# A one-core macaron block on Trainium2: GpSimd's wide SBUF operations handed to VectorE, and attention's side work spread over the query tiles

## The chip, the cores and the metric

One core of one Trainium2 chip. The metric is device time in microseconds (us) of one launch, median of several runs. The engines are TensorE (PE, with its weight loads PEld), VectorE (DVE), ScalarE (ACT), GpSimd (POOL) and SyncE (SP, which here only issues DMAs). Each engine runs its own list of instructions in order and waits on semaphores.

## The reference, cut to what matters

```python
x = x + 0.5 * ffn(layernorm(x))        # x: 4 batches x 1024 tokens x 128
x = x + attn(layernorm(x))
x = x + 0.5 * ffn(layernorm(x))
# ffn(t): logits = t Wr' + br over 8 experts; the best two, softmax of the two -> w
#         o_e = relu(t W1_e' + b1_e) W2_e' + b2_e;  result = LN(t + sum_e w_e o_e) * gamma + beta
# attn(n): q12 = n w_q12, k12 = n w_k12, v = n w_v
#          diff = softmax(q1 k1' s) - lam * softmax(q2 k2' s);  o = diff v;  o / rms(o) * 0.2
```

All is float32. The kernel computes only the two chosen experts of each token: the rows are scattered by expert into a buffer in HBM and multiplied in tiles of 128 rows.

## The kernel before, in words

A batch is 1024 tokens, held as 8 tiles of 128 (TB = 8). The program has five stages: routing of the first feed-forward (normalise rows, logits, choice of two experts, places by prefix sums, scatter of the rows by indirect DMA from POOL); the first feed-forward, 78 slots (SLOTS) of 128 rows, two groups of 39 (GSLOTS), a group holding two batches; attention over batches 0 to 3; the second feed-forward, again 78 slots; and an end that adds the results and stores them.

**A feed-forward slot** (`step`): PE transposes the rows (L842), multiplies by W1 (L850) and W2 (L860). ACT and DVE each copy half of the expert's W1 into a staging tile (L604, L1199), do half of the relus (L611, L1206), and DVE adds b2 (L1214). In the second feed-forward POOL sends each slot's result rows to HBM with an indirect DMA (`send`, L446). POOL also issues the scatters of the routed rows (`scatter`, L424), 16 to a batch. SP loads a slot's rows (`load`, L323), but those of a group only after `group_ready`: all its scatters and eight pad writes have landed. Between slots DVE takes small pieces of other work from generators (`next(...)`).

**An attention batch** (`attention(b)`, one list on each of PE, ACT and DVE, all ordered by hand). For tile i: PE computes two score matrices of 128 by 1024 (`scores`, L784 to L786, three matmuls per product); DVE takes the row maxima of each (`maxima`, L1374); ACT takes the exponentials (`probabilities`, L667), which frees the banks for the next tile's scores; DVE combines the two (`difference`, L1385); PE transposes (`turn`, L910) and ACT copies back (`dT_copy`, L641). After every four tiles PE multiplies by the keys' rows (`values`, L921) and Wv, ACT squares, POOL computes a scale (`value_scale`) and DVE adds to x (`add_values`).

Beside this, attention of batch b carries side work for its neighbours. For batch b+1: DVE merges the first feed-forward's two results per token (`merge_tiles`, tiles 0 and 1), POOL computes reciprocal roots (`rstd`, four small operations), ACT normalises, POOL multiplies by gamma and adds to x (`merge_add`, two operations on 128 by 1024), DVE takes statistics (`x_stats`, tile 5), POOL `rstd` again, ACT writes `xn` (`make_xn`), PE transposes it and multiplies by M (`turn_xn`, `multiply_M`), ACT and DVE split the products into a high and a low part (`copy_xnT`, `xnT_rest`, `copy_xm`, `xm_rest`), and then the scores of b+1 can begin. For batch b-1: `add_values(b-1, 1)` and `x_stats` in tile 4, `rstd`, `make_rows` in tile 5, transposes, logits, `choose`, `prefix` and `place` after tile 7, then POOL's scatters. For batch b+2 POOL issues 16 gathers (L435), eight of them ahead of the `rstd` that `make_rows` and `make_xn` wait for. `table(0)`, which turns the counts of batches 0 and 1 into slots, runs at the end of batch 2.

**POOL's wide operations** are four helpers, each on a whole batch (128 by 1024): `add_beta` (L416, four times in each feed-forward), `merge_add` (L462, L465), `add_tokens` (L470) and `gain` (L476). DVE waits for them through the semaphores `beta_added`, `merged`, `token_added` and `gained`.

## Time and profile before

| | us |
|---|---|
| median of three runs | 785.39 (783.78 to 787.7) |
| the profiled execution's own time | 786.02 |
| its span in the trace | 784.3 |
| busy: PE, DVE, ACT, POOL | 588.6, 518.8, 413.5, 384.9 |
| routing and first feed-forward | 0 to about 250 |
| attention | about 250 to 550 |
| second feed-forward and end | about 550 to 784 |

The trace holds one execution. A row of a timeline gives the start, the duration, the engine, the source line, the operation, output and input, the count merged into it, and in brackets how long the engine sat idle before it and what released it. Granted clock is TensorE's, 1.00 being 2.4 GHz and 0.50 being 1.2 GHz.

```profile
PE   2654599998998678976887667787989858788900
...
DVE  4654666675786786994799476853648635888726
...
POOL 6455055544453067168157313413556774666643
PEclk9955599999899999998999797998999988999965
```

These are the busy tenths in 40 slices of 19.6 us each. Attention is slices 13 to 28.

### The profile page before, as it was taken

How to read it: one execution, taken by the hardware profiler on the slowest of the kernel's cores; microseconds unless marked ns; L12 is line 12 of the kernel's file. 1: busy time of each engine (PE TensorE's matmuls, PEld its weight loads, DVE VectorE, ACT ScalarE, POOL GpSimd, SP SyncE). 2: the span in 40 equal slices, each digit the busy share in tenths (PEclk: the TensorE clock that was granted, in tenths of full speed). 3: DMA queues.
4: the chain of work that ended last, by engine and by line, in shares of the span. 5: the costliest groups of instructions: out<-in, count | busy, mean ns of one | idle time of the engine just before them, and what ended most of it. 6: DMA issues, size and time to landing. Idle time of an engine off the chain costs nothing.

```text
span 784.3 us, 16226 instructions
## 1 busy us (share of the span) xinstructions
PE 588.6 (75%) x3864; PEld 508.4 (65%) x3864; DVE 518.8 (66%) x1630; ACT 413.5 (53%) x1103; POOL 384.9 (49%) x415
## 2 busy tenths in 40 slices
PE   2654599998998678976887667787989858788900
PEld 2544599998988555554655455653988747778900
DVE  4654666675786786994799476853648635888726
ACT  3443266655556377376647644653665434646621
POOL 6455055544453067168157313413556774666643
PEclk9955599999899999998999797998999988999965
DMA  8412244324331001001000001001122321412141
GB/s 281 123 56 62 54 106 109 93 69 111 95 93 52 1 10 41 3 12 34 11 28 21 8 7 49 24 4 47 40 65 72 97 62 47 152 54 59 45 161 54
DMA packets 53677, 49.18 MB, mean 63 GB/s; under 512 B 9863, under 2 KB 45875, under 8 KB 53073
## 3 DMA queue, kind: packets, MB, share of 16 engines
q1 hardware_dynamic: 44736, 31.25, 14.6%
q0 software_dynamic: 8640, 16.87, 7.0%
q8 instruction: 35, 0.57, 0.3%
q14 instruction: 58, 0.47, 0.2%
q10 hardware_dynamic: 208, 0.02, 0.0%
HBM read 25.99 MB, written 23.02 MB: 62 GB/s over the span
## 4 chain that ended last, share of the span: by engine, by line
PE 48%; DVE 20%; issue 11%; POOL 10%; ACT 6%; DMA 3%; DVEq 1%; ACTq 0%; POOLq 0%; SPq 0%
PE banks L850 15%; PE banks L860 14%; PE banks L921 5%; PE banks L828 3%; POOL zb L435 3%; ACT rowbuf L561 2%; PE banks L842 2%; PE banks L819 2%; POOL rs L408 2%; PE banks L784 2%; POOL rows L424 2%; PE banks L786 2%; PE banks L785 2%; DVE nb L1374 1%; DVE sum_r L1241 1%
## 5 line engine op out<-in xcount | busy, mean ns | idle before, releaser
L850 PE MATMUL banks<-scratch 128*128 128x128 f32 x1248 | 174.2, 284 | 19.4 <-DVE scratch L1199 16.8
L850 PEld LDWEIGHTS banks<-scratch 128*128 128x128 f32 x1248 | 157.7, 198 | 27.0 <-issue 20.5
L860 PE MATMUL banks<-blocks,scratch 128*128 x1248 | 169.1, 280 | 0.1
L860 PEld LDWEIGHTS banks<-blocks,scratch 128*128 128x128 f32 x1248 | 156.2, 197 | 0.7 <-issue 0.5
L1206 DVE TENSOR_SCALAR scratch<-banks,blocks 128x128 f32<-128x128 f32 x312 | 95.0, 345 | 65.7 <-PE banks L850 64.5
L424 POOL DMA_INDIRECT rows<-rowbuf,slot x96 | 95.6, 996 | 67.4 <-issue 37.7
L667 ACT ACTIVATE scratch<-banks,nb 128x1024 f32<-128x1024 f32 x64 | 71.1, 1114 | 81.0 <-DVE nb L1374 80.7
L611 ACT ACTIVATE scratch<-banks,blocks 128x128 f32<-128x128 f32 x312 | 97.7, 364 | 28.5 <-PE banks L850 27.6
L598 ACT ACTIVATE scratch<-banks 128x128 f32<-128x128 f32 x156 | 43.2, 277 | 128.7 <-PE banks L842 126.4
L1374 DVE TENSOR_REDUCE nb<-banks 128x1 f32<-128x1024 f32 x64 | 76.8, 1217 | 48.1 <-PE banks L786 47.0
L446 POOL DMA_INDIRECT results<-scratch x78 | 77.7, 996 | 61.0 <-DVE scratch L1214 43.0
L435 POOL DMA_INDIRECT zb<-yrows,slot x64 | 64.8, 1012 | 53.4 <-DVE scratch L1214 25.1
L784 PE MATMUL banks<-xnTh,xmh 128*128 128x512 f32 x128 | 59.8, 467 | 36.2 <-ACT scratch L667 29.8
L1199 DVE COPY scratch<-blocks 128x256 f32 x156 | 63.4, 407 | 27.3 <-PE banks L850 18.7
L1214 DVE TENSOR_TENSOR scratch<-banks,blocks 128x128 f32<-128x128 f32 x156 | 45.0, 289 | 32.6 <-PE banks L860 23.8
L921 PE MATMUL banks<-scratch,xn 128*128 128x512 f32 x128 | 62.6, 637 | 1.5 <-ACT scratch L641 1.5
L604 ACT ACTIVATE scratch<-blocks 128x256 f32 x156 | 63.7, 408 | 0.1
L842 PE MATMUL banks<-ident,scratch 128*128 128x128 f32 x156 | 43.9, 281 | 23.5 <-issue 12.2
L784 PEld LDWEIGHTS banks<-xnTh,xmh 128*128 128x128 f32 x128 | 26.3, 205 | 48.2 <-ACT scratch L667 33.9
L424 POOL DMA_INDIRECT rows<-scratch,slot x32 | 30.5, 953 | 51.9 <-DVE scratch L1214 51.9
L786 PE MATMUL banks<-xnTh,xml 128*128 128x512 f32 x128 | 54.2, 423 | 0.0
L785 PE MATMUL banks<-xnTl,xmh 128*128 128x512 f32 x128 | 53.9, 421 | 0.0
(175 smaller groups left out, 893.0 us busy)
## 6 DMA issues: line engine op xcount, KB each, us to landing
scratch<-rows SPq DMA_DIRECT2D x156, 64.5 KB
yrows<-scratch SPq DMA_DIRECT2D x78, 64.0 KB
scratch<-results SPq DMA_DIRECT2D x3, 1024.0 KB, 7.8
rows<-padrows SPq DMA_DIRECT2D x34, 64.5 KB
x<-in_L_attn_x_dram SPq DMA_DIRECT2D x4, 512.0 KB, 6.0
scratch<-in_L_ffn_W_dram SPq DMA_DIRECT2D x1, 2048.0 KB, 19.2
out_dram<-x SPq DMA_DIRECT2D x4, 512.0 KB, 6.1
rows<-rowbuf,slot POOLq DMA_INDIRECT x96
```

The costliest lines, as they stand in the source:

```text
L424: pool.indirect_dma_start(rows[b // GB], bass.IndirectOffsetOnAxis(slot_v[:, b, j, k:k + 1], 0), rows_of(p, b)[:, j, k, :], None).then_inc ...
L435: pool.indirect_dma_start(zb[:, i * D:(i + 1) * D], None, yrows[b // GB], bass.IndirectOffsetOnAxis(slot[:, b * PAIRS + i:b * PAIRS + i + ...
L446: pool.indirect_dma_start(results, bass.IndirectOffsetOnAxis(xt_v[:, r, D:ROW].bitcast(I32), 0), ys[:, r * D:(r + 1) * D], None, bounds_ch ...
L611: ins = act.activation(hT_of(T, c), hT_at(T, c), ACT.Relu, bias=blocks[:, B1_AT + c:][:, bass.ds(at, 1)], scale=1.0)
L667: act.activation(pp, banks[:, 2 * m * 512:(2 * m + 2) * 512], ACT.Exp, bias=nb[:, 2 * i + m:2 * i + m + 1], scale=1.0, accum_out=ll[:, i:i ...
L784: pe.matmul(o, ah, bh, start=True, stop=False)
L786: return pe.matmul(o, al, bh, start=False, stop=True)
L850: ins = pe.matmul(hT_at(T, c), staged(T, c), xT_of(T), start=True, stop=True)
L860: ins = pe.matmul(y_at(T), hT_of(T, c), blocks[:, W2_AT + c * D:][:, bass.ds(at, D)], start=(c == 0), stop=(c == FC - 1))
L921: ins = pe.matmul(bank(6), xn[b % 2][:, k * D:(k + 1) * D], dT[g][:, k * QG * P:(k + 1) * QG * P], start=(k == 0), stop=(k == TB - 1))
L1206: ins = dve.tensor_scalar(hT_of(T, c), hT_at(T, c), blocks[:, B1_AT + c:][:, bass.ds(at, 1)], 0.0, ALU.add, ALU.max)
L1374: dve.tensor_reduce(nb[:, c], banks[:, 2 * m * 512:(2 * m + 2) * 512], AX_X, ALU.max, negate=True).then_inc(nb_ready, 1)
```

## The change

The four wide helpers leave POOL and run on DVE, each in two halves of 128 by 512 (`columns`), the feed-forwards' ones as generator pieces between slots. POOL's lists are reordered. In attention, side work moves: `values` of a group is issued in one piece, `add_values(b, 0)` moves into the next batch's tile 0, `add_values(b-1, 1)` and its statistics one tile earlier, `make_rows` and `make_xn` are halved over two tiles, the preparation of batch b+1 starts before tile 7's second exponential, and the logits, `choose`, `place` of batch b-1 move into batch b+1 (tiles 0 to 4); `table(0)` moves from the end of batch 2 to tile 4 of batch 3. The scores of tile 0 wait for each 512-column chunk instead of all four.

```diff
+        BETA_AT = 18
@@ POOL
-            def add_beta(p, b): ...
-            def merge_add(b): ...
-            def add_tokens(b): ...
-            def gain(b): ...
@@ POOL, first feed-forward
-                if 2 * PAIRS <= s < 2 * PAIRS + BATCHES:
-                    add_beta(0, s - 2 * PAIRS)
@@ POOL, attention
-                if b > 1:
-                    scatter(1, b - 2, range(TB))
-                if b < BATCHES - 1:
+                if b == BATCHES - 1:
+                    scatter(1, b - 3, range(10, PAIRS))
+                if after:
                     rstd(n)
                     n += 1
-                    merge_add(b + 1)
-                if b:
+                if last:
                     value_scale(b - 1, 1)
-                if b < 2:
-                    gather(b + 2, range(TB))
-                if b > 1:
-                    scatter(1, b - 2, range(TB, 2 * TB))
-                for _ in range((b > 0) + (b < BATCHES - 1)):
+                    rstd(n)
+                    n += 1
+                if after:
+                    if b < 2:
+                        gather(b + 2, range(4))
                     rstd(n)
                     n += 1
                 if b < 2:
-                    gather(b + 2, range(TB, 2 * TB))
+                    gather(b + 2, range(4, PAIRS))
+                if b == 2:
+                    scatter(1, b - 2, range(10))
+                if b == BATCHES - 1:
+                    scatter(1, b - 2)
                 value_scale(b, 0)
-            scatter(1, BATCHES - 2, range(6))
@@ POOL, second feed-forward
                 send(s)
-                if s % 2 and s < 20:
-                    i = 6 + s // 2
-                    scatter(1, BATCHES - 2, range(i, i + 1))
+                if s < PAIRS:
+                    scatter(1, BATCHES - 2, range(s, s + 1))
...
-                if s in (GSLOTS + 1, GSLOTS + 2, GSLOTS + 3, GSLOTS + 4):
-                    add_beta(1, s - GSLOTS - 1)
-                if s in (LAST_AT + 4, LAST_AT + 8):
-                    add_tokens((s - LAST_AT) // 4 - 1)
-                if s in (LAST_AT + 19, LAST_AT + 29):
-                    gain((s - LAST_AT - 19) // 10)
-            for b in range(GB, BATCHES):
-                add_tokens(b)
-            gain(2)
@@ ACT, attention
-                    probabilities(i)
+                    if last and i == 2:
+                        o_copy(b - 1, 1)
+                    if i == TB - 1:
+                        if last:
+                            copy_tgtT(a, 0)
+                        o_copy(b, 0)
+                        dT_copy(b, i - 2)
+                        if after:
+                            make_xn(b + 1, n + after + last, halves_of(1))
+                    probabilities(i, 0)
+                    if after and i == TB - 1:
+                        copy_xnT(b + 1)
+                    probabilities(i, 1)
...
+                    if b > 1 and i == 1:
+                        copy_rows(1, b - 2)
+                    if after and i in (2, 3):
+                        ins = normalise(..., n, halves_of(i - 2))
+                    if last and i in (4, 5):
+                        make_rows(1, b - 1, n + after, halves_of(i - 4))
                     if after and i == 6:
-                        make_xn(b + 1, n + after + last)
+                        make_xn(b + 1, n + after + last, halves_of(0))
@@ PE, scores
+                        if i == 0:
+                            pe.wait_ge(xmh_sb, 4 * b + 2 * m + h + 1)
+                            pe.wait_ge(xml_sb, 4 * b + 2 * m + h + 1)
@@ PE, attention
-                pe.wait_ge(xmh_sb, 4 * b + 4)
-                pe.wait_ge(xml_sb, 4 * b + 4)
...
+                    if i == TB - 1:
+                        turn(b, i - 2)
                     scores(b, i)
+                    if b > 1 and i == 0:
+                        logits(a - 1)
...
+                    if last and i == 1:
+                        values(b - 1, 1, 0)
+                        values(b - 1, 1, 1)
+                    if last and i == 2:
                         multiply_Wv(b - 1, 1)
+                    if b > 1 and i == choose_tile(b) + 1:
+                        prefix(a - 1)
...
                 multiply_Wv(b, 0)
                 if after:
-                    pe.wait_ge(xnTh_sb, b + 2)
-                    pe.wait_ge(xnTl_sb, b + 2)
+                    multiply_M(b + 1)
                 turn(b, TB - 2)
-                if after:
-                    multiply_M(b + 1)
@@ DVE
+            def add_beta(p, b):      # two pieces of 128 x 512, then beta_added
+            def gain(r):             # two pieces
+            def merge_add(b):
+                dve.wait_ge(scaled, b)
+                at_once(gain(sum_r))
+                dve.wait_ge(beta_added, b + 1)
+                for q in range(2): ... dve.tensor_tensor(x[:, c], x[:, c], sum_r[...], ALU.add)
@@ DVE, last_sums / last_add: the tokens' sum and the gain, two pieces each, ahead of the rest
@@ DVE, attention
                     maxima(i)
+                    if after and i == TB - 1:
+                        xnT_rest(b + 1)
                     if i:
                         difference(i - 1)
+                    if b > 1 and i == 0:
+                        read_logits(a - 1)
+                    if last and i == 0:
+                        add_values(b - 1, 0)
...
+                    if b > 1 and i == choose_tile(b):
+                        at_once(choose(a - 1))
-                    if last and i == 4:
+                    if last and i == 3:
                         add_values(b - 1, 1)
                         x_stats(b - 1, n)
+                    if b > 1 and i == choose_tile(b) + 2:
+                        at_once(place(a - 1, b - 2))
+                    if b == BATCHES - 1 and i == 4:
+                        at_once(table(0))
                     if after and i == 5:
-                        dve.wait_ge(merged, b + 1)
+                        merge_add(b + 1)
                         x_stats(b + 1, n)
+                if after:
+                    xm_rest(b + 1)
                 difference(TB - 1)
...
@@ DVE, feed-forwards
+                if BETA_AT <= s < BETA_AT + 2 * BATCHES:
+                    next(first_betas)
-                    if LAST_AT + 7 + 10 * f <= s < LAST_AT + 16 + 10 * f:
+                    if LAST_AT + 5 + 10 * f <= s < LAST_AT + 16 + 10 * f:
                         next(ending[f], None)
-                    if LAST_AT + 22 + 10 * f <= s < LAST_AT + 24 + 10 * f:
+                    if LAST_AT + 20 + 10 * f <= s < LAST_AT + 24 + 10 * f:
                         next(adding[f], None)
+                if GSLOTS - 8 <= s < GSLOTS - 8 + 2 * BATCHES:
+                    next(last_betas)
```

`choose_tile(b)` is 2 for batch 2 and 0 for batch 3.

## Rows read from the trace of the kernel before

**Rows 1.** The page's part 4: shares of the chain by engine.

```profile
PE 48%; DVE 20%; issue 11%; POOL 10%; ACT 6%; DMA 3%; DVEq 1%; ACTq 0%; POOLq 0%; SPq 0%
```

**Rows 2.** Windows, one per attention batch: width, busy by engine, clock, DMA share, GB/s.

```profile
260.00:317.00 57.00, 43.70 (x197) 31.74 (x198) 45.38 (x97) 36.45 (x69) 29.64 (x29) 0.97 0.07 19
317.00:389.00 72.00, 56.43 (x257) 41.02 (x258) 54.61 (x135) 44.84 (x92) 33.18 (x36) 0.95 0.06 15
389.00:464.00 75.00, 57.63 (x257) 41.97 (x257) 56.93 (x149) 45.24 (x93) 34.27 (x36) 0.91 0.04 15
464.00:536.00 72.00, 54.39 (x245) 39.76 (x244) 49.28 (x124) 37.63 (x73) 21.27 (x26) 0.90 0.07 23
```

**Rows 3.** Timeline of DVE in attention, batches 0 and 1.

```profile
290.13 2.55 DVE L1374 TENSOR_REDUCE nb<-banks 128x1 f32<-128x1024 f32 x2
...
293.09 1.29 DVE L1385 SCALAR_TENSOR_TENSOR scratch<-scratch,cc 128x1024 f32<-128x1024 f32 x1
...
339.24 3.46 DVE L1385 SCALAR_TENSOR_TENSOR scratch<-scratch,cc 128x1024 f32<-128x1024 f32 x1
...
371.71 1.22 DVE L1374 TENSOR_REDUCE nb<-banks 128x1 f32<-128x1024 f32 x1 [10.52 <-PE banks L786]
...
392.86 2.35 DVE L1374 TENSOR_REDUCE nb<-banks 128x1 f32<-128x1024 f32 x2
```

**Rows 4.** Timeline of POOL in batch 1: the two operations of `merge_add`.

```profile
339.27 2.36 POOL L462 TENSOR_TENSOR sum_r<-sum_r,gammab 128x1024 f32<-128x1024 f32 x1 [4.35 <-ACT sum_r L561]
341.71 3.25 POOL L465 TENSOR_TENSOR x<-x,sum_r 128x1024 f32<-128x1024 f32 x1
```

**Rows 5.** Timelines of ACT (first row) and PE in attention.

```profile
361.62 3.18 ACT L561 ACTIVATE rowbuf<-x,nm,rs 128x128 f32<-128x128 f32 x8 [6.27 <-POOL nm L410]
...
260.07 0.47 PE L784 MATMUL banks<-xnTh,xmh 128*128 128x512 f32 x1 [1.50 <-DVE xml L1354]
...
364.86 1.12 PE L819 MATMUL banks<-ident,rowbuf 128*128 128x128 f32 x4 [6.01 <-ACT rowbuf L561]
```

**Rows 6.** Groups by shape: DVE's addition of 128 by 512 from two SBUF tiles.

```profile
L1339 DVE TENSOR_TENSOR x<-x,scratch 128x512 f32<-128x512 f32 x4 | 2.7, 688 | 3.7 <-issue 2.9 <-POOL scratch L476 0.7
```

**Rows 7.** Timeline of DVE in the feed-forwards, beside POOL's wide operations.

```profile
164.39 1.73 DVE L1199 COPY scratch<-blocks 128x256 f32 x1
...
665.23 2.90 DVE L1199 COPY scratch<-blocks 128x256 f32 x1
...
668.77 2.91 DVE L1199 COPY scratch<-blocks 128x256 f32 x1
...
682.34 0.61 DVE L1206 TENSOR_SCALAR scratch<-banks,blocks 128x128 f32<-128x128 f32 x2 [0.23 <-PE banks L850]
683.23 0.29 DVE L1214 TENSOR_TENSOR scratch<-banks,blocks 128x128 f32<-128x128 f32 x1 [0.28 <-PE banks L860]
683.72 0.29 DVE L1199 COPY scratch<-blocks 128x256 f32 x1 [0.20 <-PE banks L850]
...
694.38 3.42 DVE L1241 SCALAR_TENSOR_TENSOR sum_r<-zb,wts,sum_r 128x128 f32<-128x128 f32 x2
...
720.11 3.27 DVE L1241 SCALAR_TENSOR_TENSOR scratch<-scratch,wts 128x128 f32<-128x128 f32 x2
```

**Rows 8.** Timelines of PE (first, last) and POOL, second feed-forward, first group.

```profile
571.96 0.74 PE L819 MATMUL banks<-ident,rowbuf 128*128 128x128 f32 x4 [3.06 <-ACT rowbuf L561]
...
642.66 0.98 POOL L446 DMA_INDIRECT results<-scratch  x1 [0.30 <-issue]
643.94 0.97 POOL L424 DMA_INDIRECT rows<-rowbuf,slot  x1 [0.31 <-issue]
...
649.52 0.45 PE L842 MATMUL banks<-ident,scratch 128*128 128x128 f32 x1 [12.24 <-issue]
```

**Rows 9.** Timeline of the end: POOL's and DVE's operations on the last two batches.

```profile
758.26 2.33 POOL L470 TENSOR_TENSOR scratch<-scratch,tgt 128x1024 f32<-128x1024 f32 x1 [8.59 <-ACT scratch L713]
...
760.63 4.65 DVE L1241 SCALAR_TENSOR_TENSOR scratch<-scratch,wts 128x128 f32<-128x128 f32 x8 [13.58 <-POOL scratch L470]
```

More of the change, by code:

```diff
@@ L275, in macaron_kernel, with halves_of, choose_tile @@
         LAST_AT = GSLOTS + 6
+        def halves_of(tiles):
+            return range(tiles * TB // 2, (tiles + 1) * TB // 2)
+        def choose_tile(b):
+            return 0 if b == BATCHES - 1 else 2
         def wait_apart(eng, *waits):
@@ L1242, in second_result, with columns @@
                 return ins
+            def columns(b, piece, pieces):
+                n = TB * D // pieces
+                return slice(b * TB * D + piece * n, b * TB * D + (piece + 1) * n)
+            def add_beta(p, b):
+                dve.wait_ge(rows_ready, BATCHES * p + b + 1)
+                for q in range(2):
+                    xq = x[:, columns(b, q, 2)].rearrange("p (j d) -> p j d", d=D)
+                    ins = dve.tensor_tensor(xq, xq, betab[:, :].unsqueeze(1).broadcast_to([P, TB // 2, D]), ALU.add)
+                    if q:
+                        ins.then_inc(beta_added, 1)
+                    yield
+            def gain(r):
+                for q in range(2):
+                    rq = r[:, columns(0, q, 2)].rearrange("p (j d) -> p j d", d=D)
+                    steps.then(dve.tensor_tensor(rq, rq, gammab[:, :].unsqueeze(1).broadcast_to([P, TB // 2, D]), ALU.mult))
+                    yield
+            def merge_add(b):
+                dve.wait_ge(scaled, b)
+                at_once(gain(sum_r))
+                dve.wait_ge(beta_added, b + 1)
+                for q in range(2):
+                    c = columns(b, q, 2)
+                    ins = dve.tensor_tensor(x[:, c], x[:, c], sum_r[:, columns(0, q, 2)], ALU.add)
+                steps.then(ins)
             def merge_tiles(b, tiles):
@@ L1319, in last_sums @@
                 pairs = [range(j, j + 2) for j in range(0, TB, 2)]
-                dve.wait_ge(token_added, b + 1)
+                dve.wait_ge(weighted, b + 1)
+                for q in range(2):
+                    steps.then(dve.tensor_tensor(sums[b][:, columns(0, q, 2)], sums[b][:, columns(0, q, 2)], tgt[:, columns(b, q, 2)], ALU.add))
+                    yield
                 for t in pairs:
@@ L1333, in last_add @@
             def last_add(b):
-                dve.wait_ge(gained, b + 1)
-                dve.wait_ge(beta_added, BATCHES + b + 1)
-                for h in range(2):
-                    c = slice(b * TB * D + h * TB * D // 2, b * TB * D + (h + 1) * TB * D // 2)
-                    ins = dve.tensor_tensor(x[:, c], x[:, c], sums[b][:, h * TB * D // 2:(h + 1) * TB * D // 2], ALU.add)
-                    if h:
+                dve.wait_ge(scaled, BATCHES + b)
+                yield from gain(sums[b])
+                for q in range(2):
+                    c = columns(b, q, 2)
+                    ins = dve.tensor_tensor(x[:, c], x[:, c], sums[b][:, columns(0, q, 2)], ALU.add)
+                    if q:
                         ins.then_inc(x_done, 1)
@@ L1445, in _ @@
             merging = first_merge(n)
+            first_betas = itertools.chain(*(add_beta(0, b) for b in range(BATCHES)))
+            last_betas = itertools.chain(*(add_beta(1, b) for b in range(BATCHES)))
             finding = [find(b) for b in range(BATCHES)]
```

119 lines of the change are left out of this document (45 added, 74 removed).

## The prediction, made before the changed kernel ran

> **What bounds the kernel now.** I read the chain of waits first. PE holds not quite half of it, DVE a fifth, and POOL a tenth [rows 1]. POOL's tenth is the part to look at, since this change empties it. Next come the windows, one per attention batch: batch 1 lasts 72.0 us with PE busy 56.4, DVE 54.6 and POOL 33.2; batch 2 lasts 75.0 with 57.6, 56.9 and 34.3 [rows 2]. No engine is full, and two are nearly equal, so the batch pays for waits between engines. The DVE timeline shows what a tile costs when nothing waits: the two maxima start at 290.13 and the difference ends at 293.09 + 1.29 = 294.38, so 4.25 us a tile and 34 for eight [rows 3]. It also shows two holes in batch 1. DVE waits 10.52 us ahead of tile 7, and from tile 7's maxima (371.71) to the next batch's last one of tile 0 (392.86) 21.2 us go by [rows 3].
>
> The ACT and PE timelines name the first hole: ACT stood 6.27 us for POOL's `nm` before `make_rows`, and PE 6.01 us for ACT [rows 5]. POOL was late because `merge_add` took 339.27 to 344.96 [rows 4] and eight gathers stood between it and the `rstd`. Batch 2 shows the same wait. The second hole is the hand-over, done in a row after tile 7: transposes, product with M, split into parts, `choose`, `place`. In it PE waits 1.50 us for the last `xml` chunk before tile 0's scores, once per batch [rows 5].
>
> In the feed-forwards a clean slot lasts 1.90 us, and DVE has 0.23 + 0.28 + 0.20 = 0.71 us of waiting in it [rows 7]. Beside POOL's `add_beta` the copy L1199 lasts 2.91 instead of 0.29, and slots follow each other by 668.77 - 665.23 = 3.54 [rows 7].
>
> The sums below are against the profiled execution's own time, 786.02, 0.6 above the median of 785.39.
>
> **First feed-forward.** `add_beta` leaves POOL. DVE's copies there grew only to 1.73 (three of them, the others 1.25 and less) [rows 7]: each loses 1.44 less the 0.71 of slack, so 0.7, and all about 1.2. Eight pieces of 128 by 512 come to DVE, each 0.69 [rows 6], one to a slot, and 0.69 fits in 0.71. **-1.2**; if the cover were short by the issue of each, 8 x 0.2 would make it +0.4.
>
> **Attention.** Off the path: the late `rstd`. POOL's list now has `rstd` directly after at most four gathers; four at 1.28 apart [rows 8] are 5.1 us, and they run while DVE does tiles 4 and 5. Of the 10.5 us hole I take 9 as gone; what is late next is ACT, with 3.2 us of `make_rows` [rows 5] now in halves. DVE's difference that lasted 3.46 in place of 1.29 beside the POOL multiplication returns 2.2 [rows 3, 4].
>
> The hand-over, followed: `xn` is ready before tile 7's exponentials; then `copy_xnT`, `xnT_rest` (1.2), product with M, four `xml` pieces (2.5), the two last differences (3.2): some 11 us from tile 7's first maximum to the next batch's first, against 21.2 less the second maximum's 1.2 and 1.1, so 19. But `choose` and `place` (3.5 and 3.3 by the same timeline) are only moved, into tiles 2 and 4 (0 and 2 of batch 3), and stand before the next maxima there. So -8 for each hand-over, and 6.8 of it given back in a batch that routes: batches 2 and 3. Batch 1 routes nothing now.
>
> Added: DVE gets four pieces per `merge_add`, 4 x 0.69 = 2.8 us [rows 6], in three batches, at tile 5, where `x_stats` (2.4) follows. PE covers part: its `values` of tile 6 (about 6.9 us at full clock) lies there, so scores and maxima of tile 6 are late rather than PE idle. I charge half, bounds none and all. DVE's new wait for `scaled` has the next tile's maxima behind it, but ACT's normalising is in tiles 2 and 3, two tiles ahead. The wait of `o_copy` ahead of tile 2's exponentials costs nothing: that tile's scores are queued behind the same `values`. `values` in one piece makes DVE wait 1.4 us at tile 2.
>
> By batch. DVE's work is the floor [rows 2, 6]: batch 1 54.6 + 2.8 - 2.2 = 55.2. Following the three lists tile by tile I get 60; seven or so hops between engines of 0.2 us, of which I left some out, make it 62, so -9.9. Batch 2: 66 by hand, 68 with hops, against 75: -7. Batch 0 has no hole: 56 against 56.8, -0.8. Batch 3 with the end of attention, up to the second feed-forward's first slot at 549.5: 84.5 against 86.2, -1.7. The chunk waits give 1.5 once more at the start. Sum **-21**. Bounds: by hand without hops -27; with `merge_add` charged in full (+4.2) and each moved piece of routing also costing a stall (two batches of 3.5) -10.
>
> **Second feed-forward, first group.** POOL sends and scatters at 1.28 us apiece (643.94 - 642.66) [rows 8], 2.56 a slot against 1.90, and the group cannot begin before the last scatter: PE idles 12.24 us until 649.52 [rows 8]. This stall stays. Six scatters that ran before slot 0 now run inside slots 0 to 15: 6 x 1.28 = 7.7 us more for POOL, but POOL had waits for DVE in slots 0 to 19 that take most of it. Three of them stand before the `rstd` of batch 3, which PE already waits for (3.06 us idle at 571.96 [rows 8]); that wait grows by 2.5. I take **+2**, bounds 0 and +7.7. DVE's eight `add_beta` pieces in slots 31 to 38 are hidden: PE waits for POOL there.
>
> **Second group.** `add_beta`: four slots at 3.54 become 1.90: 4 x 1.64, less the first one's shorter growth: -6.3. `add_tokens`: a difference piece of 3.42 in place of 0.6 [rows 7] and a copy of 2.09 in place of 0.29, with 1.2 more where the clock fell: -5.8 in all; its pieces on DVE, 4 x 0.69, fit the slack: +0.3. `gain`: 3.27 in place of 0.6 [rows 7]: -2.7. The last `gain` stood before the last three sends: 2.4 less the slots' own end, -1.8. Given back: slots in which the ends of both batches have a piece, 1.4 us against 0.71, four to six of them: +2. The group: **-14.3**, bounds -16 and -8.
>
> The Trainium skill bears on this. "SBUF — State Buffer", section "Who interferes with whom", says that DVE and GpSimd take a shared port pair by an exclusive lock, and that a DVE `tensor_tensor` with both inputs in SBUF contends with GpSimd's reads. The rows of 2.91, 3.42 and 3.46 agree with the first half. The second half speaks against the change: the additions and gains are such operations, so each could still wait for a POOL operation. By the rule a piece that meets an `rstd` (about 2.6 us on this trace, most of it one operation) waits for it; with one such meeting in each of the two last parts the sum would be 751, without it 749. Which of the two holds for an addition of two SBUF tiles beside POOL's short operations no row here shows.
>
> **The end.** Before, POOL's sum of the tokens of batch 2 runs 758.26 to 760.59, and DVE's eight operations take 4.65 because the next sum on POOL stretches one of them by 2 [rows 9]. After: two pieces of 0.7 on DVE, then eight in 2.6. That is 1.4 + 2.6 = 4.0 in place of 2.3 + 4.65 = 7.0, less batch 3's own 1.4 now on DVE, and the `gain` of batch 2 (2.3 on POOL behind the last `rstd`) becomes 1.4 on DVE: **-2.4**, bounds -3.5 and -1.
>
> **Sum:** 786.0 - 1.2 - 21 + 2 - 14.3 - 2.4 = 749.1 for the profiled execution, 748.5 on the scale of the median; I say 749.
>
> **Rivals.**
> *The waits move, attention gains half.* DVE goes from 208 us of work in attention to some 212, in fewer us, and every side piece stands in front of a maximum, with the exponential and the next scores behind. For it: tiles 0 and 1 of each batch, where DVE already carries the merge, have PE idle 2.5 to 4.2 us each by the PE timeline; the change makes such tiles of 3, 4 and 5 too. Against: the two holes are 30 us of batch 1 alone [rows 3]. Attention -10 or less: 749 + 11 = 760, up to 768.
> *The lists mesh better.* Attention reaches the hand-followed -27, and POOL's longer list costs 0: 749 - 8 = 741.
> *Slower: the clock.* Granted clock in attention is 0.97, 0.95, 0.91 and 0.90 by batch [rows 2], lower where PE's idle gaps are. If many short idle gaps in place of few long ones kept PE at 1.2 GHz for long, PE would bind: busy 43.7 + 56.4 + 57.6 + 54.4 = 212 us at a mean of 0.93 [rows 2]. It cancels the gain of 37 when 212 x (0.93 / c - 1) = 37, so c = 0.79; at 0.75 it is +51, or 800. Against: with fewer idle us PE has been denser, and the sparsest batch (batch 0, 13 us idle) has the highest clock.
> *A new wait takes most of it back:* POOL's 16 scatters of batch 1 now run after the `rstd` in batch 3 (20 us). If they ended after attention, SP's loads and the first slot would wait up to 20.4 + 4 = 24: 773. By hand they end 40 us before it.
>
> **How the numbers follow.** Forecast with its own range 745 to 757: 0.52. Attention gains little (757 to 770): 0.22. Better mesh (735 to 745): 0.17. Most taken back (770 to 781): 0.04. The clock, slower: 0.03; and 0.02 for no net effect. The range 738 to 768 leaves out about a fifth. Less than 0.5% (4 us) can't be told from no change here. Faster 0.94, same 0.02, slower 0.04.
>
> **What would show it.** DVE's L1199 never over 1.3 us in either feed-forward; no DVE idle over 4 us before tile 7; first maximum of batch b+1 within 13 us of the first maximum of tile 7; attention near 268 us instead of 290; PE's 12 us stall before the second group still there, POOL's last scatter of it at most 4 us later relative to slot 0; the last PE work to the end shorter by 2. Wrong would be idle of 3 us or more before scores in most tiles, or a granted clock under 0.85 in attention.

## The result, and the profile after

The changed kernel takes **752.9 us** (median of 4 runs, 749.8 to 755.0) where the kernel before takes 786.5 (4 runs, 783.8 to 787.7): ratio **0.957 [0.954, 0.961]**, faster. The forecast was 749, with a range of 738 to 768: right in sign, size and range. The profiled execution of the changed kernel took 754.97, span 753.2; the sum in the prediction was made for such a one and gave 749.1.

Cut at the same places of both programs, the two profiled executions differ so (us; I cut at starts of PE's work in the timelines):

```
stage                                    before   after   change   forecast
up to the first product with W2            93.5    93.3    -0.2       0
first feed-forward                        160.5   158.0    -2.5      -1.2
attention                                 293.5   269.8   -23.7     -21
second feed-forward, first group          102.1   107.5    +5.4      +2
second group, to PE's last product         96.1    89.4    -6.7     -12.5
PE's last product to the end               38.7    35.2    -3.5      -4.2
```

(The -1.8 of the last sends, which the prediction had in the second group, is in the last row here, where it falls.)

The page after: busy time, and the shares of the chain by engine, which answer to [rows 1].

```profile
PE 583.5 (77%) x3864; PEld 506.8 (67%) x3864; DVE 517.6 (69%) x1672; ACT 413.3 (55%) x1103; POOL 336.1 (45%) x394
...
PE 47%; DVE 25%; issue 10%; POOL 7%; ACT 6%; DMA 4%; SPq 1%; DVEq 1%; ACTq 0%; POOLq 0%
```

DVE took 42 more instructions and is busy no longer than before (517.6 us against 518.8): what it lost by standing beside POOL's wide operations pays for what it was given.

Attention's windows, which answer to [rows 2] (width, busy by engine, clock, DMA share, GB/s):

```profile
253.00:311.00 58.00, 45.98 (x197) 33.37 (x197) 47.12 (x97) 35.70 (x63) 18.53 (x21) 0.93 0.06 14
311.00:370.00 59.00, 50.86 (x237) 36.38 (x236) 51.67 (x124) 42.26 (x89) 28.24 (x34) 1.00 0.07 19
370.00:435.00 65.00, 54.59 (x258) 39.86 (x257) 57.66 (x153) 45.31 (x93) 22.93 (x30) 0.97 0.04 13
435.00:510.00 75.00, 59.12 (x274) 44.43 (x273) 56.13 (x147) 42.46 (x87) 32.53 (x36) 0.89 0.09 29
```

In batch 2 DVE now works 57.7 of 65.0 us where it worked 56.9 of 75.0. DVE's timeline around the hand-over from batch 0 to 1 and from 1 to 2, which answers to [rows 3]; at the end the same wait in batch 3:

```profile
302.85 2.58 DVE L1404 TENSOR_REDUCE nb<-banks 128x1 f32<-128x1024 f32 x2 [3.09 <-PE banks L772]
...
314.31 2.35 DVE L1404 TENSOR_REDUCE nb<-banks 128x1 f32<-128x1024 f32 x2
...
361.63 2.58 DVE L1404 TENSOR_REDUCE nb<-banks 128x1 f32<-128x1024 f32 x2 [3.11 <-PE banks L772]
...
373.55 2.35 DVE L1404 TENSOR_REDUCE nb<-banks 128x1 f32<-128x1024 f32 x2
...
494.04 2.58 DVE L1404 TENSOR_REDUCE nb<-banks 128x1 f32<-128x1024 f32 x2 [7.52 <-PE banks L772]
```

In batch 1 tile 7's maxima wait 3.1 us, not 10.5. In batch 3 the hole stayed: 7.5 us, where the kernel before has 6.4. The next batch's first maxima begin 11.5, 11.9 and 11.9 us after tile 7's. In the kernel before the same three distances are 17.2, 21.2 and 25.5; the prediction has 19 for the second of them, because it took 392.86 for the second maximum of tile 0, and that row starts with the first.

The second feed-forward's first group, POOL, ACT and PE before batch 3's transposes, which answers to [rows 8]:

```profile
543.27 0.25 POOL L417 TENSOR_SCALAR rs<-mv 128x8 f32<-128x8 f32 x1
...
545.64 0.20 POOL L420 TENSOR_SCALAR nm<-nm 128x8 f32<-128x8 f32 x1
545.94 1.65 ACT L536 ACTIVATE rowbuf<-x,nm,rs 128x128 f32<-128x128 f32 x4 [4.47 <-POOL nm L420]
...
550.15 1.12 PE L805 MATMUL banks<-ident,rowbuf 128*128 128x128 f32 x4 [6.21 <-ACT rowbuf L536]
...
623.03 0.97 POOL L428 DMA_INDIRECT rows<-rowbuf,slot  x1 [0.30 <-issue]
...
628.61 0.45 PE L829 MATMUL banks<-ident,scratch 128*128 128x128 f32 x1 [12.31 <-issue]
```

Read it from the fourth row upwards: PE is idle 6.21 us, not 3.06, because ACT stood 4.47 us for POOL's `nm`, and POOL's `rstd` had five scatters of this stage ahead of it. In the kernel before it had two. The last operation of `rstd` starts 24.5 us after the group's first transpose, and 20.0 in the kernel before.

The second group: SP's load of the first group's results, and who stands for it (ACT, PE, DVE).

```profile
646.92 0.33 SPq L377 DMA_DIRECT2D zb<-results  x1
650.35 0.29 DVE L1210 TENSOR_TENSOR scratch<-banks,blocks 128x128 f32<-128x128 f32 x1 [0.28 <-PE banks L847]
...
652.58 0.69 ACT L699 ACTIVATE sum_r<-zb,wts 128x128 f32<-128x128 f32 x2 [4.85 <-DMA zb<-results]
653.58 0.30 PE L829 MATMUL banks<-ident,scratch 128*128 128x128 f32 x1 [3.37 <-ACT scratch L573]
656.26 0.61 DVE L1202 TENSOR_SCALAR scratch<-banks,blocks 128x128 f32<-128x128 f32 x2 [5.12 <-PE banks L837]
657.75 0.29 DVE L1210 TENSOR_TENSOR scratch<-banks,blocks 128x128 f32<-128x128 f32 x1 [0.88 <-PE banks L847]
...
663.12 0.68 DVE L1349 TENSOR_TENSOR sum_r<-sum_r,tgt 128x512 f32<-128x512 f32 x1
```

L1210 marks the slots: between two of them lie 657.75 - 650.35 = 7.40 us where a clean slot has 1.90, so the load costs 5.5. In the kernel before ACT stood only 2.05 us at that place, inside the last of the stretched slots, and each of the next six slots lasted 1.9. The pieces of `add_tokens` on DVE (last row) take 0.68 each and stretch nothing.

The end, which answers to [rows 9]:

```profile
729.83 1.42 DVE L1349 TENSOR_TENSOR scratch<-scratch,tgt 128x512 f32<-128x512 f32 x2 [10.78 <-ACT scratch L699]
731.28 2.56 DVE L1237 SCALAR_TENSOR_TENSOR scratch<-scratch,wts 128x128 f32<-128x128 f32 x8
```

### The profile page after: what moved, and what is told of

It reads as the page before. It is cut to its first block, busy times and chain, and to the rows that moved or that the text cites. A ratio compares the mean times of both kernels' runs of the same rounds, so it can differ in the third digit from the quotient of the medians.

```text
span 753.2 us, 16264 instructions
## 1 busy us (share of the span) xinstructions
PE 583.5 (77%) x3864; PEld 506.8 (67%) x3864; DVE 517.6 (69%) x1672; ACT 413.3 (55%) x1103; POOL 336.1 (45%) x394
## 4 chain that ended last, share of the span: by engine, by line
PE 47%; DVE 25%; issue 10%; POOL 7%; ACT 6%; DMA 4%; SPq 1%; DVEq 1%; ACTq 0%; POOLq 0%
PE banks L837 16%; PE banks L847 14%; DVE nb L1404 5%; POOL zb L439 4%; PE banks L914 3%; PE banks L814 3%; PE banks L770 2%; PE banks L829 2%; DVE st_x L1057 2%; DVE scratch L1415 2%; PE banks L771 2%; PE banks L772 2%; PE banks L805 1%; DMA results<-scratch 1%; DVE mv L1063 1%
## 5 line engine op out<-in xcount | busy, mean ns | idle before, releaser
L586 ACT ACTIVATE scratch<-banks,blocks 128x128 f32<-128x128 f32 x312 | 97.4, 363 | 18.5 <-PE banks L837 17.2
L439 POOL DMA_INDIRECT zb<-yrows,slot x64 | 66.6, 1041 | 61.1 <-issue 37.6
L770 PE MATMUL banks<-xnTh,xmh 128*128 128x512 f32 x128 | 57.0, 445 | 30.4 <-ACT scratch L642 30.4
L1210 DVE TENSOR_TENSOR scratch<-banks,blocks 128x128 f32<-128x128 f32 x156 | 45.0, 288 | 29.9 <-PE banks L847 21.1
L417 POOL TENSOR_SCALAR rs<-mv 128x8 f32<-128x8 f32 x20 | 5.3, 267 | 133.4 <-DVE mv L1063 132.9
L1195 DVE COPY scratch<-blocks 128x256 f32 x156 | 47.4, 304 | 25.1 <-PE banks L837 15.7
L829 PE MATMUL banks<-ident,scratch 128*128 128x128 f32 x156 | 44.2, 283 | 25.8 <-issue 12.3
L914 PE MATMUL banks<-scratch,xn 128*128 128x512 f32 x128 | 57.9, 606 | 1.1 <-ACT scratch L616 1.1
```

What stands on the lines that cost most here:

```text
L439: pool.indirect_dma_start(zb[:, i * D:(i + 1) * D], None, yrows[b // GB], bass.IndirectOffsetOnAxis(slot[:, b * PAIRS + i:b * PAIRS + i + ...
L586: ins = act.activation(hT_of(T, c), hT_at(T, c), ACT.Relu, bias=blocks[:, B1_AT + c:][:, bass.ds(at, 1)], scale=1.0)
L770: pe.matmul(o, ah, bh, start=True, stop=False)
L914: ins = pe.matmul(bank(6), xn[b % 2][:, k * D:(k + 1) * D], dT[g][:, k * QG * P:(k + 1) * QG * P], start=(k == 0), stop=(k == TB - 1))
```

## The experiments

All twelve kernels ran later than the first comparison, in three groups, each with the kernel before beside it: e1 to e4 on a chip with the number 11, the others on one with the number 10. The number of the first comparison's chip is not on record. In all three groups the kernel before takes 828.8 to 829.5 us, not 786.5. These are called the later runs here, and each kernel is read by its ratio to the kernel before of its own group. No ratio among them is as far as 2.5% from 1, so small differences are at stake.

**The two kernels again.** Both were run unaltered, the kernel before for its trace.

> The changed kernel itself, unaltered, so that the other kernels of this group have it beside them on the same chip. Theory A (the state of the chip stretches both kernels in proportion): ratio to the kernel before 0.957, as in the first comparison; with the kernel before at 786 that is 752, with it at 829 it is 794. Theory B (on the chip of the earlier experiments the change itself gains less, since five of its variants lay between 0.992 and 0.997 there): if the kernel before is at 829 again, this one is at 820 to 828, ratio 0.99 to 0.998.

> The kernel before, unaltered, for its trace on this chip. Theory A (this chip runs it as the first did): 786 us, with attention at 293.5, the second feed-forward's first group at 102 and routing before the first tile's weights at 93.5. Theory B (this chip adds stalls that the first did not): about 829 us, with the first stretch at 107 to 111, attention near 296 and the first group near 126, as in the variants run there.

Measured: the changed kernel 823.9 (12 runs, 818.3 to 827.1) against 828.8 (17 runs): **0.992 [0.989, 0.995]**. The kernel before, one run, 831.2. Theory B holds, in both. The stages in the later runs (the last two columns are kernels told of below):

```
stage                        before   changed   e2_pool_order   f3_pool_late
up to the first W2 product    107.2    106.8        106.9           106.9
first feed-forward            165.3    163.5        162.8           164.1
attention                     293.9    286.8        284.2           290.6
second, first group           124.6    133.7        125.3           121.8
second group                  100.6     94.0         92.0            93.7
end                            37.8     35.3         35.0            35.6
```

Each column is one execution, and these lie 2.4 above, 2.1 below, 5.0 below and 1.8 us above the medians of their kernels. Attention's lists on PE, ACT and DVE are the same in the last three columns, and its row still differs by 6.4. A difference of a few us in one row shows nothing by itself.

DVE and ACT are busy for as long as in the first comparison (the changed kernel: DVE 516.6 and 517.6, ACT 411.0 and 413.3). PE is busy for longer: 610.8 us at a mean granted clock of 0.875, against 583.5 at 0.900. The rest is idle time, with waits whose releaser the profile does not show. In the changed kernel's timeline of the later runs, PE, ACT and DVE in a slot of the second feed-forward's first group:

```profile
589.13 0.27 PE L829 MATMUL banks<-ident,scratch 128*128 128x128 f32 x1
...
594.85 0.28 ACT L573 ACTIVATE scratch<-banks 128x128 f32<-128x128 f32 x1 [6.27 <-remote]
...
595.27 0.45 PE L829 MATMUL banks<-ident,scratch 128*128 128x128 f32 x1 [3.98 <-issue]
...
596.51 0.61 DVE L1202 TENSOR_SCALAR scratch<-banks,blocks 128x128 f32<-128x128 f32 x2 [5.07 <-remote]
```

The transpose that ACT copies had been done since 589.4. Such waits belong to places in the program, and not to one chip: ACT's copy of slot 50 of the first feed-forward waits 5.1 in the changed kernel on chip 10 and 5.2 in e1_zs_early on chip 11, that of slot 6 of the second 5.7 in both, and 0.7 at both places in the first comparison. In the changed kernel DVE has 107 us of idle time without a shown releaser in the later runs, ACT 106; in the first comparison 10 and 8.

In the kernel before attention takes as long in the later runs as in the first comparison (293.9 and 293.5), in the changed one 17 us longer. The hand-overs hold most of it. Their three distances (tile 7's first maxima to the next batch's) add up to 63.8 us in the kernel before and 63.9 in f2_before, but to 35.3 in the changed kernel of the first comparison and 49.4 in f1_control, and to 46.3 to 48.8 in the eight other kernels of the later runs that have the changed attention. The split of the product with M is where they lengthen. ACT's copies of batch 1, first comparison, then f1_control:

```profile
309.21 2.70 ACT L609 ACTIVATE xmh<-banks 128x512 fp32r<-128x512 f32 x4 [1.24 <-PE banks L772]
```

```profile
326.01 0.60 ACT L609 ACTIVATE xmh<-banks 128x512 fp32r<-128x512 f32 x1 [1.23 <-PE banks L772]
328.53 0.60 ACT L609 ACTIVATE xmh<-banks 128x512 fp32r<-128x512 f32 x1 [1.93 <-PE banks L772]
332.06 0.60 ACT L609 ACTIVATE xmh<-banks 128x512 fp32r<-128x512 f32 x1 [2.93 <-remote]
333.49 0.60 ACT L609 ACTIVATE xmh<-banks 128x512 fp32r<-128x512 f32 x1 [0.83 <-remote]
```

Four copies take 2.7 us in the one and 8.1 in the other, though PE had finished all four products by 328.1. In the kernel before the same four take 2.5 both times. So these waits are new in the changed order, and the gain of 28.5 us that the hand-overs gave in the first comparison is 14.5 in the later runs. Part of that gain is taken back by the pieces that moved into the tiles. The granted clock differs too: in attention it is 0.94 and 0.90 in the changed kernel, with PE busy 221.9 and 233.5 us, and 0.92 and 0.91 in the kernel before, with 227.4 and 232.8. What the waits are was not tested. Nor is it shown that the chip makes the difference, since the first comparison's chip is not known.

**The halves of the change.** First the kernel before with only the feed-forwards' helpers (`add_beta`, `add_tokens`, `gain`) in pieces on DVE; then the changed kernel's attention with helpers and POOL's order in the feed-forwards as before.

> The kernel before with only the feed-forwards' wide helpers (beta, the tokens' sum, gamma) on DVE, in the changed kernel's slots; attention, merge_add on POOL and POOL's order as before. Theory (by stage from the two traces: first feed-forward -2.7, second group -6.7, end -3.5, and no loss in the first group): 13 us under before, 773.5. Rival (the rest of the -33 comes from here, since contention is the main thing): 765 or less.

> The changed kernel's attention (lists of PE, ACT, DVE and POOL, merge_add on DVE) with the feed-forwards' helpers on POOL and POOL's scatter order as before. Theory: attention alone gives 23.7 us: 762.5. Rival (attention's gain needs the helpers off POOL too, or most of it is variation): over 767.

Measured: helpers alone 820.4, **0.988 [0.985, 0.990]**; attention alone 823.7, **0.993 [0.990, 0.995]**. So -9.1 and -5.8; both gain, each less than was expected from the first comparison. Their sum is -14.9, and the whole change has -4.8. What is in the whole and in neither half is POOL's order in the second feed-forward.

**POOL's order.** The changed kernel with the scatters of batch 2 as the kernel before has them:

```diff
+            scatter(1, BATCHES - 2, range(6))
             value_scale(BATCHES - 1, 1)
...
-                if s < PAIRS:
-                    scatter(1, BATCHES - 2, range(s, s + 1))
+                if s % 2 and s < 20:
+                    i = 6 + s // 2
+                    scatter(1, BATCHES - 2, range(i, i + 1))
```

> The changed kernel with POOL's scatters of batch 2 placed as before: six ahead of slot 0, ten in the odd slots up to 19. Theory (the first group lost time through POOL's list: the reciprocal root of batch 3 behind five scatters instead of two, and six more indirect DMAs inside the slots): the idle time of PE before the transposes of batch 3 falls from 6.2 to about 3.1 us, and the stretch from the first slot to the second group's first from 105.5 to about 100.5 us: 748. Rival (the longer stretch comes from DVE's eight additions in slots 31 to 38): no change, 753, and the stretch stays at 105 us.

And with eight scatters ahead of slot 0 and eight in slots 5 to 12, behind the `rstd` of slot 4:

```diff
+            scatter(1, BATCHES - 2, range(8))
             value_scale(BATCHES - 1, 1)
...
-                if s < PAIRS:
-                    scatter(1, BATCHES - 2, range(s, s + 1))
+                if 5 <= s < 13:
+                    scatter(1, BATCHES - 2, range(s + 3, s + 4))
```

> The changed kernel with only GpSimd's order altered: of batch 2's sixteen scatters eight go ahead of slot 0, into GpSimd's 21 us of idleness there, and eight into slots 5 to 12, behind the short power chain of slot 4. My reading: that chain no longer waits behind five scatters, so the matmul stall of 6.2 us before batch 3's transposes shrinks to about 3 and the first group is 3 to 5 us shorter: ratio to the control 0.994 to 0.996, 748 to 750 where the control is at 753. Rival (the order is immaterial, scatters only end earlier or later): same as the control within 0.2%.

Measured: e2_pool_order 813.0, **0.980 [0.976, 0.983]**; f3_pool_late 812.6, **0.978 [0.973, 0.982]**, beside 0.992 [0.989, 0.995] of the changed kernel (f3_pool_late in the same group, e2_pool_order on the other chip). -16.4 for the first is near the -14.9 of the two halves. So the order costs 11 us in the later runs, and the first group's row of the table is where it shows most (133.7 against 125.3 and 121.8). The intervals don't meet that of the changed kernel: the rival "immaterial" falls, and so does the rival of DVE's eight additions in slots 31 to 38, which are in all three. The two times are level, and the lowest of the later runs. POOL in f3_pool_late, and PE behind it:

```profile
568.64 1.06 POOL L450 DMA_INDIRECT results<-scratch  x1 [3.70 <-DVE scratch L1211]
...
580.66 0.20 POOL L420 TENSOR_SCALAR nm<-nm 128x8 f32<-128x8 f32 x1
...
585.17 0.66 PE L806 MATMUL banks<-ident,rowbuf 128*128 128x128 f32 x4 [2.18 <-issue]
```

and the same places in f1_control:

```profile
565.54 1.07 POOL L450 DMA_INDIRECT results<-scratch  x1 [5.13 <-DVE scratch L1210]
...
583.94 0.20 POOL L420 TENSOR_SCALAR nm<-nm 128x8 f32<-128x8 f32 x1
...
588.64 0.66 PE L805 MATMUL banks<-ident,rowbuf 128*128 128x128 f32 x4 [1.62 <-issue]
```

From POOL's first send to the end of `nm` it is 18.6 us in the changed kernel and 12.2 in f3_pool_late: five scatters of 1.27, as expected. But PE's own wait before the transposes is no shorter (2.18 and 1.62), and the gain is more than twice what I expected, so my reading of where it comes from does not hold in the later runs. ACT's copies of the token tiles tell where it lies (start of the copy of a slot in the first group, after that of slot 0):

```
slot                                 6      10      20      38
changed, first comparison          11.6    24.8    51.2    91.8
before, first comparison           10.2    20.3    46.0    86.5
f1_control                         16.6    27.3    65.8   123.8
f2_before                          14.1    23.5    54.1   115.1
e2_pool_order                      14.0    23.5    53.8   114.9
f3_pool_late                       10.2    19.4    54.2   111.8
```

f2_before and e2_pool_order, which share POOL's order here but not the helpers' engine nor attention's lists, agree within 0.3 us, on two chips. Against f3_pool_late, 6.4 of the changed kernel's 12 us are there by slot 6, where ACT's wait of 5.7 without releaser stands; against e2_pool_order it is 2.6 of 8.9, and most comes between slots 10 and 20. Slot 6 is the later the more scatters run in slots 0 to 5 (six, three, none). That is a correlation of a few kernels, and no more. In the first comparison slot 6 is only 1.4 late, and 3.1 of the rest comes between slots 6 and 10, where PE's longer wait for the transposes is.

**The load of the results.** SP issues it four slots earlier, in the changed kernel and in f3_pool_late:

```diff
-                if s == GSLOTS + 10:
+                if s == GSLOTS + 6:
                     all_sent(0)
```

> The changed kernel, with SP issuing the loads of the first group's results at slot 45 of its own list instead of 49; nothing else differs. Theory (the results land late): in the changed kernel ACT sat 4.85 us for that load at 652.58, and DVE's b2 additions stand 7.4 us apart there instead of 1.9; four slots earlier is 7.6 us, so the wait goes and the run is 5 to 5.5 us shorter than the changed kernel (752.9), about 747.5; second group 84 us instead of 89.4. Rival (slots there are slow for DVE's extra pieces, the load wait only falls into them): no more than 1.5 us shorter, 751.5 or more.

> The same order of GpSimd, and the load of the first group's results issued four slots earlier (slot 6 of the second group instead of slot 10). My reading: the 4.85 us wait of ScalarE for that load, and the 5.5 us that TensorE loses behind it, go: a further 4 to 5 us, 743 to 746 where the control is at 753. Rival (an earlier load arrives while gathers and stores of the same queue are under way and blocks SyncE's sends instead): within 1 us of the kernel with the order alone.

Measured: e1_zs_early 824.8, 0.994 [0.993, 0.996]; f4_pool_late_zs 814.0, 0.980 [0.976, 0.985]. Neither is told apart from its partner (0.992 and 0.978), so the readings by which 4 to 5.5 us go fell. The rivals come near: e1 is 0.9 us over f1_control, and f4 is 1.4 over f3_pool_late, where its rival says within 1. f1_control (ACT and PE), then f4_pool_late_zs (SP, PE and ACT):

```profile
714.42 0.69 ACT L699 ACTIVATE sum_r<-zb,wts 128x128 f32<-128x128 f32 x2 [3.74 <-DMA zb<-results]
...
715.41 0.30 PE L829 MATMUL banks<-ident,scratch 128*128 128x128 f32 x1 [2.27 <-ACT scratch L573]
```

```profile
689.60 0.32 SPq L377 DMA_DIRECT2D zb<-results  x1
...
699.34 0.47 PE L830 MATMUL banks<-ident,scratch 128*128 128x128 f32 x1 [4.77 <-DMA scratch<-rows]
...
704.86 0.69 ACT L700 ACTIVATE sum_r<-zb,wts 128x128 f32<-128x128 f32 x2
```

ACT's wait is gone, and PE waits 4.77 us for token rows instead (5.28 in e1_zs_early). SP issues no row load from 687.5 to 691.5 (for 1.9 us around the load in f3_pool_late): it stands in `all_sent` and issues the large load, and the row loads come behind. The slot with the load lasted 4.8 us in f1_control and 3.8 in f3_pool_late; the slot that waits for rows lasts 9.3 in e1_zs_early and 9.0 here. A load moved along its queue took its stall with it, and made it longer.

**`add_beta` of the second group back on POOL.** In slots 40 to 43, as the kernel before has it; alone, and with the early load.

```diff
+                if s in (GSLOTS + 1, GSLOTS + 2, GSLOTS + 3, GSLOTS + 4):
+                    add_beta(1, s - GSLOTS - 1)
...
-                if GSLOTS - 8 <= s < GSLOTS - 8 + 2 * BATCHES:
-                    next(last_betas)
```

> The changed kernel with the last four additions of beta back on POOL (slots 40 to 43) and off DVE. Theory: the stretched copies cost 6.3 us in those slots, but the same 6.3 us let the load of the results land before ACT asks for it, so the wait of 5.5 us goes and the whole is 0 to 2 us longer than the changed kernel: 753 to 755. Rival (the stretch and the load wait are independent): 6.3 us longer, 759.

> The same with the load of the results also issued at slot 45. Theory: nothing is hidden any longer by the stretch, so it costs 6 us against the kernel with the early load alone: 753.5, and the same as the one without the early load. If the stretch cost nothing, it would be 747.5 as that one.

Measured: 825.5, 0.993 [0.990, 0.996]; with the early load 825.7, 0.994 [0.991, 0.997]. The first is 1.5 us over the changed kernel, inside the intervals: the rival of 6.3 us longer falls. The second was to cost 6 us against the early load alone, and has 0.9, since the early load alone gained nothing. DVE's timeline of e3_beta_pool has the long copies again, one of them here:

```profile
706.55 2.91 DVE L1203 COPY scratch<-blocks 128x256 f32 x1
```

Its four slots are 6 us longer, and yet the thirteen slots from 39 to 52 take 32.7 us against 30.8 in f1_control: 1.9. Of the 4.2 that come back, 2.9 are the slot in which ACT now finds the results loaded; slot 51 is 1.8 shorter by waits without a shown releaser, and other slots are 0.5 longer. About half of the gain of taking `add_beta` off POOL here is given back to the load.

**`merge_add` alone.** Once back on POOL in the changed kernel, behind the early `rstd`; once to DVE in the kernel before.

```diff
                 if after:
+                    merge_add(b + 1)
                     if b < 2:
                         gather(b + 2, range(4))
...
-                        merge_add(b + 1)
+                        dve.wait_ge(merged, b + 1)
```

> The changed kernel with merge_add back on POOL, behind the reciprocal root of the batch before; all lists otherwise as changed. Theory (the order of the side work gives the gain; the wide operations themselves cost DVE as much when they collide as they save it): within 4 us of the changed kernel, 751 to 757. Rival (taking the wide operations off POOL gives attention's gain): most of the 23.7 us is lost, 768 or more.

> The kernel before with only merge_add moved to DVE (four pieces of 128 by 512 in tile 5). Theory of order: DVE gains 8.4 us of work and loses two stretches of 2.2, POOL's chain is 5.7 us shorter in each batch, but eight gathers still stand ahead of the reciprocal root: 1 to 5 us shorter than before, 782 to 785. Rival (moving is what counts): 15 us or more shorter, 771 or less.

Measured: back on POOL 826.6, **0.996 [0.994, 0.999]**, so 2.7 over the changed kernel, with intervals that overlap; to DVE alone 832.6, **1.003 [1.000, 1.005]**. The engine alone gains nothing: e8 is 3.1 us longer where 1 to 5 shorter was expected, so attention's gain needs the new order of the lists. How much of it needs the move as well stays open. The rival of e7 gave the move 15 us or more, and in the later runs all of attention gains only some 6 to 7; 2.7 of that may be the move's. In e7 the hand-overs add up to 48.8 us, as with the move, so their gain does not hang on it.

## Why the prediction was right, and where its terms were off

**First feed-forward, -1.2:** -2.5. No copy L1195 lasts over 0.53 us in either feed-forward; small, and right in sign. The prediction counts three stretched copies of 1.73; the trace has two, and one each of 1.25 and 0.76.

**Attention, -21:** -23.7. The forecast's batches run from PE's first product for tile 0 to the next one's, the last to the first slot's second transpose. By these marks (255.64, 311.91, 371.14, 436.09, 523.11) they last 56.3, 59.2, 65.0 and 87.0 against forecasts of 56, 62, 68 and 84.5. So two batches gained more than forecast, and batch 3 lost 1.3 where a gain of 1.7 was forecast: its tiles 0 and 3 last 7.1 and 7.5 us, which lasted 5.5 and 4.5, with the pieces of routing that moved there, and the hole before its tile 7 stayed at 7.5. There the sign "no DVE idle over 4 us before tile 7" failed.

The mechanism held where it was said to pay: the hole before tile 7 of batch 1 shrank by 7.4, not 9, and the hand-over went to 11.5 and 11.9 as followed. But it came down from 17.2, 21.2 and 25.5, so it gave 28.5 us in three, not 8 each. The 2 us of hops that I added to batches 1 and 2, each, were not needed. `merge_add` on DVE was charged by half, 1.4 a batch, and cost all of it: from tile 5's maxima to tile 6's it is 9.3, 9.3 and 9.1 us, and 6.5, 6.3 and 6.3 in the kernel before; in e7_merge_pool it is 6.3 in all three again. That the sum came out within 2.7 is in part luck: these misses have both signs.

e8 shows that the engine of `merge_add` alone gains nothing. That the order is the cause in the first comparison rests on the waits named in its two traces; the attention by itself (e6_attn_only) gave 5.8 in the later runs, where attention's row has -7.1 instead of -23.7.

**Second feed-forward, first group, +2:** +5.4, inside the bounds of 0 and 7.7. The step was right and mis-sized. Three more scatters stand before the `rstd` (five where there were two), as I had counted; I took 2.5 for them where three at 1.28 are 3.8, and the wait for `make_rows` grew by 3.15 (6.21 for 3.06). Another 1.4 is there by slot 6, which I had not named. POOL's waits in the later slots, which I let absorb the rest, did not: the last scatter came 101.9 us after the first transpose instead of 96.5, 5.4 later, where I had said at most 4. PE's 12.3 us stall stayed, as said. e2 and f3 show that the order costs 11 us in the later runs, a part of it ahead of the `rstd`, by a way that I had not named. Neither ran beside the first comparison; its two traces give the 3.15.

**Second group, -14.3:** with the last sends where they fall, -12.5 was forecast and -6.7 measured. The pieces did what was said: no stretched copy, 0.68 a piece. The missing term is the wait for the load of results, 5.5 us in one slot. Before, the stretched slots of `add_beta` and the load ran side by side, so I should have asked, when the slots shorten by 6.3, what was due behind them. [Rows 7] show only what goes; the SP row was not looked at. e3 tells the same from the other side: with `add_beta` back, 6 us of stretch cost 1.9, and the slot of the load is 1.9 again.

**The end, -2.4, with the -1.8 of the last sends:** -3.5 for the two. DVE's tokens and sums take 1.42 + 2.56 = 3.98 for batch 2, as worked out (4.0).

**The sum** missed by 5.9 (749.1 against 754.97): +5.8 in the second group and +3.4 in the first, less 2.7 of attention and smaller terms.

The rule of the Trainium skill, "SBUF — State Buffer", section "Who interferes with whom", was weighed in the prediction. Its lock agrees with the 2.91 us copies, gone with POOL's wide operations and back in e3. For the additions and gains of two SBUF tiles the trace has DVE at its usual 0.68 to 0.71 an operation beside POOL's short operations, and POOL as the one that waits. POOL at the end:

```profile
739.28 0.20 POOL L419 TENSOR_TENSOR nm<-mv,rs 128x8 f32<-128x8 f32 x1
...
745.06 0.71 POOL L419 TENSOR_TENSOR nm<-mv,rs 128x8 f32<-128x8 f32 x1
745.86 0.63 POOL L420 TENSOR_SCALAR nm<-nm 128x8 f32<-128x8 f32 x1
```

and DVE beside the last two:

```profile
745.02 1.42 DVE L1259 TENSOR_TENSOR scratch<-scratch,gammab 128x512 f32<-128x512 f32 x2
746.47 1.29 DVE L1369 TENSOR_TENSOR x<-x,scratch 128x512 f32<-128x512 f32 x2
```

So 0.5 us on POOL, and none on DVE: the forecast without such meetings was the better one. In these two meetings the DVE operation had started first, and each POOL operation ended just after it. In e7_merge_pool one began the other way round. POOL's long operation of the last `rstd`, and DVE's gain that starts inside it:

```profile
815.08 1.85 POOL L418 TENSOR_TENSOR rs<-rs,nhalf 128x8 f32<-128x8 f32 x1
```

```profile
816.76 1.42 DVE L1269 TENSOR_TENSOR scratch<-scratch,gammab 128x512 f32<-128x512 f32 x2
```

DVE's pair starts right behind DVE's operation before it (which ends at 816.72) and takes its usual 1.42, so the long operation did not hold it either.

**What stays open:** why the later runs have waits that no row names, at fixed places of the program; whether the chip, or something else that differs between the sets of runs, brings them; and what f3_pool_late would bring where the first comparison ran.

## What to carry over

When wide operations leave a slot, list what was running in parallel with the slots that shorten, loads on other queues first: that is what is late next, and moving it up its queue only moves the stall. Price in full what is put in a queue before a short operation that others wait for: three more scatters at 1.28 us were taken for 2.5 here. Compare the parts of a forecast by the marks that it was made with, since a sum can be near while its terms miss on both sides. And a gain that comes from closing waits can be taken back by other waits: the same change gave 4.3% in one set of runs and 0.8% in another, so run both kernels beside each experiment.

## What the runs showed of the hardware

- The same program takes 786.5 us in one set of runs and 829 in three later ones, on two chips. In the profiled executions of the kernel before, the granted clock is 0.895 and 0.881, PE is busy 588.6 and 608.6 us, DVE 518.8 and 517.5, ACT 413.5 and 411.8; the rest of the difference is idle time.
- A DVE operation on two SBUF tiles lengthens POOL's short operations beside it by up to 0.5 us (0.71 and 0.63 instead of 0.20), and is itself not lengthened.
- POOL's issue of an indirect DMA takes 0.97 us, and up to 1.48 where it begins while DVE works on two SBUF tiles of 128 by 512 (698.66, 700.66 and 718.51 in the changed kernel: 1.41, 1.48 and 1.38).
